# A query's weight rest and statistics placed ahead of a group of context rests on VectorE (cross attention over a long context, one core)

## The reference

```python
ln_out = _ln(hidden_states, ln_w, ln_b)
q  = _ln(_fp8_linear(ln_out, wq));  k = _ln(_fp8_linear(ln_out, wk));  v = _fp8_linear(ln_out, wv)
core = _gqa(q, k, v)                       # 16 query heads, 8 key heads, over the 64 own tokens
qx = _ln(_fp8_linear(ln_out, wqx))
kx, vx = split(einsum('bsi,oi->bso', cond, w_kv_x))   # cond: 1601 context rows
kx = _ln(kx)
xout = _gqa(qx, kx, vx)                    # over the 1601 context rows
catq = _div_clamp_fp8(concatenate([core, xout]), proj_smooth)
return einsum('bsi,oi->bso', catq, wproj) * (proj_in_scale * proj_w_scale)
```

## Time and profile before

| what | value |
|---|---|
| median of 3 runs | 1945.05 us (1943.37 to 1945.61) |
| the profiled execution, its own time | 1945.92 us |
| its span | 1944.6 us |
| TensorE busy | 1869.5 us, 96% |
| VectorE, ScalarE, GpSimd busy | 1187.0 (61%), 910.9 (47%), 731.2 us (38%) |
| attention loop, first to last score product | 138 to 1699 us, some 24.4 us a step |

### The profile page before, as it was taken

How to read it: one execution, slowest core, us unless ns; L and a number is a source line. 1 busy time by engine, 2 the same in 40 slices (tenths; PEclk the granted TensorE clock), 3 DMA queues, 4 the chain that set the end, 5 groups by cost and what they waited for, 6 DMA issues and landing times.

```text
span 1944.6 us, 31175 instructions
## 1 busy us (share of the span) xinstructions
PE 1869.5 (96%) x10065; PEld 1588.2 (82%) x10065; DVE 1187.0 (61%) x3161; ACT 910.9 (47%) x1892; POOL 731.2 (38%) x806
## 2 busy tenths in 40 slices
PE   6899999999999999999999999999999999998968
PEld 5777888888888888888888888888888888875357
DVE  7765566656565566556655765566556755546853
ACT  6653444545554555444544554455445544335611
POOL 4236554433333333334444444444444344301010
PEclk9999999999999999999999999999999999999979
DMA  8674354534453454435453544455435533474020
GB/s 276 228 251 144 106 157 133 175 114 145 149 173 120 123 171 141 152 91 178 131 155 113 171 149 140 117 175 160 142 114 180 162 114 103 154 255 165 3 87 22
DMA packets 221890, 283.82 MB, mean 146 GB/s; under 512 B 61025, under 2 KB 123746, under 8 KB 221730
## 3 DMA queue, kind: packets, MB, share of 16 engines
q1 hardware_dynamic: 211090, 280.86, 45.8%
q10 hardware_dynamic: 8592, 0.54, 0.3%
q0 software_dynamic: 2048, 0.43, 0.1%
HBM read 241.98 MB, written 39.22 MB: 145 GB/s over the span
## 4 chain that ended last, share of the span: by engine, by line
PE 78%; DVE 5%; ACT 4%; DMA 3%; issue 2%; POOL 0%; ACTq 0%; SPq 0%; DVEq 0%; POOLq 0%
PE u_ps L630 9%; PE kx_ps L524 8%; PE u_ps L633 8%; PE kx_ps L526 8%; PE kx_ps L528 8%; PE u_ps L632 8%; PE t_ps L616 4%; DMA stage<-in_ctx_n 3%; PE sc_ps L601 3%; PE sc_ps L603 2%; PE sc_ps L602 2%; PE ssq_ps L543 2%; PE t_ps L657 2%; PE t_ps L640 1%; DVE ctxN_lo L298 1%
## 5 line engine op out<-in xcount | busy, mean ns | idle before, releaser
L524 PE MATMUL kx_ps<-ctxT_hi,wk_hi 128*128 128x400 f32 (+1 forms) x1024 | 364.6, 356 | 5.5 <-DVE ctxT_lo L298 5.5
L526 PE MATMUL kx_ps<-ctxT_lo,wk_hi 128*128 128x400 f32 (+1 forms) x1024 | 354.5, 346 | 0.0
L528 PE MATMUL kx_ps<-ctxT_hi,wk_lo 128*128 128x400 f32 (+1 forms) x1024 | 353.4, 345 | 0.0
L630 PE MATMUL u_ps<-ctxN_hi,pt_hi 128*128 128x512 f32 x832 | 340.6, 409 | 6.9 <-DVE pt_lo L855 6.9
L633 PE MATMUL u_ps<-ctxN_hi,pt_lo 128*128 128x512 f32 x832 | 329.0, 395 | 0.0
L632 PE MATMUL u_ps<-ctxN_lo,pt_hi 128*128 128x512 f32 x768 | 304.4, 396 | 0.0
L855 DVE TENSOR_TENSOR pt_lo<-t_ps,pt_hi 128x512 fp32r<-128x512 f32 (+1 forms) x256 | 144.6, 588 | 242.2 <-ACT pt_hi L1120 242.2
L1089 ACT ACTIVATE kx_hi<-kx_ps 128x400 fp32r<-128x400 f32 (+1 forms) x256 | 128.8, 503 | 304.7 <-PE kx_ps L528 303.1
L1120 ACT ACTIVATE pt_hi<-t_ps 128x512 fp32r<-128x512 f32 (+1 forms) x256 | 126.0, 524 | 254.6 <-PE t_ps L616 254.5
L782 DVE TENSOR_TENSOR kx_lo<-kx_ps,kx_hi 128x400 fp32r<-128x400 f32 (+1 forms) x256 | 146.7, 573 | 151.5 <-ACT sq L1091 149.8
L524 PEld LDWEIGHTS kx_ps<-ctxT_hi,wk_hi 128*128 128x128 f32 x1024 | 193.8, 189 | 10.9 <-DVE ctxT_lo L298 6.0
(11 more groups left out here) (286 smaller groups left out, 3663.0 us busy)
## 6 DMA issues: line engine op xcount, KB each, us to landing
rstd_bc<-scratch_rstd SPq DMA_DIRECT2D x64, 804.0 KB, 6.0
stage<-in_ctx_n SPq DMA_DIRECT2D x104, 256.0 KB, 6.4
stage<-in_ctx_t SPq DMA_DIRECT2D x96, 267.0 KB, 4.6
wk_hi<-scratch_wk_s SPq DMA_DIRECT2D x56, 256.0 KB, 3.0
wk_lo<-scratch_wk_s SPq DMA_DIRECT2D x56, 256.0 KB, 3.5
wv_hi<-scratch_wv_s SPq DMA_DIRECT2D x56, 256.0 KB, 4.9
wv_lo<-scratch_wv_s SPq DMA_DIRECT2D x56, 256.0 KB, 5.8
scratch_own_rows<-out_sb SPq DMA_DIRECT2D x32, 256.0 KB, 2.8
```

The costliest lines, as they stand in the source:

```text
L524: PE.matmul(kx_ps[:, j % 2, 0:w], wk_hi[:, g % 2, i, :], ctxT_hi[:, i, c0:c0 + w], start=(i == 0), stop=False)
L526: PE.matmul(kx_ps[:, j % 2, 0:w], wk_hi[:, g % 2, i, :], ctxT_lo[:, i, c0:c0 + w], start=False, stop=False)
L528: mm = PE.matmul(kx_ps[:, j % 2, 0:w], wk_lo[:, g % 2, i, :], ctxT_hi[:, i, c0:c0 + w], start=False, stop=(i == C - 1))
L630: PE.matmul(u_ps[:], pt_hi[:, t % 2, cols], ctxN_hi[:, y, :], start=(y == 0), stop=False)
```

## The change

In VectorE's list of a step the call `refill(1)`, the rests of the pieces of place 1, moves behind the block with `query_low(n + 1)` and `query_stats(n + 2)`. It still stands in front of `values_out(n)`. The lists of the other engines are not changed.

```diff
                 if v:
                     prob_low(n, 2)
                     prob_low(n, 3)
-                refill(1)
                 if v and s:
                     query_low(n + 1)
                     if r:
                         query_stats(n + 2)
+                refill(1)
                 if v:
                     values_out(n)
                 if s:
```

## The result

| what | before | after |
|---|---|---|
| median of 4 runs each | 1945.33 us (1943.37 to 1945.84) | 1934.24 us (1932.30 to 1935.96) |
| ratio, 95% interval | 1 | 0.9949 (0.9936 to 0.9961) |
| the profiled execution, own time and span | 1945.92, 1944.6 us | 1935.84, 1933.8 us |
| last value product of n = 0 to that of n = 62 | 1529.16 us | 1518.06 us |

What follows compares the result with a forecast made beforehand. TensorE, busy in 96% of the span, was taken as the bound, so only its waits could be saved. Term 1 (-8.9) and terms 2 and 3 (-3.2) made -12.1 us, for a median of 1933.0 us, range 1928.5 to 1938.0.

Steps and rivals of the forecast that it cites:

- Rival A: Own forecast for the loop: `q_lo` waits go, steps n % 8 = 0 gain a little; 1933.0 us, chance 0.57.
- Term 1: Steps n % 8 = 5 or 7: first score product no longer waits for `q_lo`, `u_sb` not late; -8.9 us.
- terms 2 and 3: Steps n % 8 = 0: fewer `pt_lo` waits less new stalls, -7.3 + 3.8 = -3.5, taken as -3.2 us.
- Rival D: Steps n % 8 = 5 or 7: next VectorE user holds the step, nothing gained; 1945 us, chance 0.10.
- Term 2: Earlier statistics and `rstd_bc` load land the awaited context piece earlier, ending `pt_lo` waits at n % 8 = 0; up to -7.3 us.
- Term 3: Steps n % 8 = 0: last context piece's rest, behind `query_low`, makes TensorE wait; at most +3.8 us.
- part 2: Same as Term 2: earlier statistics, `rstd_bc` and awaited piece; bounds 0 and -7.3 us.
- signs of being wrong: Rests start later than ScalarE's copies allow, awaited piece keeps its landing time, or `q_hi` slips at n % 8 = 0.
- B: Only the `q_lo` gain in steps n % 8 = 5 or 7 works; 1936.1 us, chance 0.18.
- C: Gains of -8.9 and -7.3 us in full, `q_hi` in time at every n % 8 = 0; 1928.9 us, chance 0.08.
- E: Slower: at n % 8 = 0 `query_low` holds VectorE until `q_hi`, 2.2 us each; 1951.6 us, chance 0.07.

Runs made afterwards that it cites:

- low_only: Against the kernel before, only `query_low` moves ahead of the rests of place 1, `query_stats` stays behind them; 1941.28 us, ratio 0.9969.
- stats_only: Against the kernel before, only `query_stats` moves ahead of the rests of place 1, `query_low` stays behind them; 1943.19 us, ratio 0.9982.
- stats_last: The change, but with n % 8 of 5 or 7 `query_stats` goes behind the second scaling of scores; 1958.74 us, 1.0063 of the kernel before.
- rstd_later_old: Kernel before, with SyncE's `rstd_bc` load behind the piece of place 5 at n % 8 = 7 and in the entry step; 1936.39 us, ratio 0.9963.
- rstd_later: The change, plus SyncE's `rstd_bc` load behind the piece of place 5 at n % 8 = 7 and in the entry step; 1930.43 us, ratio 0.9921.
- own_behind: The change, plus GpSimd's `own_norm` moved behind `query_high` of the next step; 1930.07 us, 0.9932 of the kernel before.
- not_zeros: The change everywhere but in steps with n % 8 = 0, which keep the old order; 1934.36 us, 0.9937 of the kernel before.
- all_four: The change with `rstd_later` (not in the entry step), `make_later` and `own_behind` together; 1927.31 us, 0.9917 of the kernel before.
- zeros_only: Against the kernel before, the new order only in steps with n % 8 = 0; 1946.54 us, ratio 1.0004.
- make_later: The change, plus VectorE's first `ternary_make` moved behind later rests in odd steps from n = 29; 1932.83 us, 0.9943 of the kernel before.

## Why the prediction was right

**Time.** 1933.0 us was forecast, from 1928.5 to 1938.0; 1934.24 us was measured. Rival A held. Term 1, four fifths of the gain, came out by its mechanism and its size; that terms 2 and 3 came out near in their sum was luck.

**Term 1, -8.9 us: right in size, -8.83.** Its steps are those of the rows: `q_lo` 2.3 us ahead, the statistics inside the idle time, the rests unmoved, `u_sb` at +0.43. The two steps that I had taken 0.4 us off for, n = 23 and 29, stand at 3.25 and 3.30 us where the others take 3.03 to 3.06. What I had not seen is that the statistics carry 3.9 us of it. My sum was right, since it counted TensorE's whole delay against n = 22; my reading of the wait, as one for `q_lo` alone, was not, and `low_only`, for which I expected 8.8, showed it. Even when `q_lo` is early, statistics that stand behind the rests keep `u_sb` late by 0.4 us. Rival D is refuted by the same rows.

**Term 2, up to -7.3 us: the mechanism is shown, the size was too large.** `stats_only` and `stats_last` show the chain from the statistics over GpSimd, `rstd_bc` and SyncE's queue to the piece awaited in the zero; `rstd_later_old` shows its last link alone. But 7.3 us was more than there is: with every wait out of the zeros Z is -6.3. The 0.26 us that I put on top of each wait came from one wait of a score product, and the zeros don't have it: their seven waits for `pt_lo` and three that I had not counted, for the squares of the keys (0.25 to 0.49 us in n = 8, 16 and 24), are 6.5 us as noted, of which 6.3 come back. And the step "so the piece should land about 2 us earlier against TensorE" held in four zeros (2.1 to 2.3 us in n = 8, 16, 24 and 56) and not in n = 32, 40 and 48 (0.8, 1.2 and 0.9 us), where ScalarE still idles for 1.9 to 2.2 us and not for less than 0.5. `rstd_bc` was to be issued 5.3 us after the last value product in the sevens and is issued after 6.0 to 7.4 us. Two things took the lead away. First `q_n`, in all sevens and fives: it takes 0.80 us in every step of the loop before, and 1.53 to 1.88 us in the 14 fives and sevens after. There, and only there, it runs while VectorE takes the context rests (533.77 to 535.06 in n = 15). By the Trainium skill, "SBUF — State Buffer", section "Who interferes with whom", this is what a VectorE instruction with two SBUF inputs does to GpSimd; the trace agrees in part: `q_n` is 0.73 to 1.08 us longer, in n = 15 0.74 us over an overlap of 1.0 us, where I had given 1.3 us as the upper case. Second, the small store of the key norms lands later in n = 31, 39 and 47 (3.3, 2.7 and 3.2 us after its issue), the sevens ahead of just those three zeros, and in no other seven; the transfers in a short window around it, in n = 31 (the packets of each queue: number, MB, share; then KB each and us from issue to landing) and in n = 15:

```profile
q8 instruction: 1, 0.02, 1.6%
...
scratch_rstd<-rstd_col POOLq DMA_DIRECT2D x1, 6.5 KB, 3.3
```

```profile
scratch_rstd<-rstd_col POOLq DMA_DIRECT2D x1, 6.5 KB, 1.8
```

3.3 us against 1.8 us from issue to landing, and `rstd_bc` waits for it: 7.42 us after the last value product in place of 6.01. Why it lands late is not shown by an experiment (below).

**Term 3, +3.8 us: the mechanism is right, the size was too large.** The wait of a value product for the piece's rest exists, in one zero (1.0 us, n = 56), and in five when the transfers are helped (`rstd_later`). `own_behind` puts what `q_hi` takes back after the change at 1.6 us at most, 0.9 of it in n = 56; `not_zeros` doesn't tell the cost of the order from nothing. It was smaller for two reasons. In n = 32, 40 and 48 part 2 gave less, as I had allowed for. And n = 8, which I had counted with the late ones, is not of their kind after the change: `q_hi` comes 0.7 us earlier against TensorE's keys there, and the piece's rest follows ScalarE's copy. One of my signs of being wrong was that `q_hi` slips in the zeros; in n = 56 it did, by 0.4 us. Two terms too large of opposite sign made a net that is near by cancelling: -3.2 us forecast for 2 and 3, -3.05 measured. That net is luck.

**The remaining rivals.** B (only part 1) is refuted by `stats_only`; in the four late zeros the change comes close to it, 0.56 us of gain. C is about what `all_four` reaches in the loop (-8.87 - 6.32), by three more edits and not by itself. E's place, `query_low` ahead of the last piece in the zeros, is there, but `zeros_only` and `not_zeros` show at most 0.3 us for it in sum, and not 1.8 us a zero. The other places lost 0.8 us. The largest are 0.63 us from n = 61 to 62 and 0.58 us from n = 12 to 13, where a wait of 0.5 us for `pt_lo` is new; both scatter from kernel to kernel (the second from 0.1 to 1.1 us).

## What to carry to other kernels

When two independent instructions of an in-order engine move together, ask for each of them who waits for it: here the one read as the cause brought 4.9 us, the small one behind it 3.9 us more where it stood and up to 6 us three engines and one step further on. A result that another engine turns into a transfer belongs ahead of work that nobody awaits, and its lateness is not symmetrical: 2.7 us earlier brought 3 to 6 us in the zeros, 1.5 us later (2.1 us against TensorE) cost 16. When a wait ends because something comes earlier, look up what is due next in that step (`q_hi` here) before counting the whole wait as gain.

## What the runs showed that I had not expected

- **The same GpSimd instruction took twice the time behind the start of a context rest:** `q_n` 0.80 us in all steps of the loop before, 1.53 to 1.88 us in the 14 steps where it starts while one runs. In `stats_only` it starts 0.2 us ahead of the rests in n = 23 and 29; there it takes 0.80 us, and the first of the two rests takes 0.80 us against 0.68 and 0.70 for the second. The 14 take 22.5 us together where 14 x 0.80 = 11.2 us would do, which is 11.3 of the 14.7 us by which GpSimd's busy time grew.
- **A 6.5 KB store issued by GpSimd lands after 1.8 us, or up to 4.0 us after its issue.** In the loops of the kernel before, the change, `stats_only` and `make_later` it landed later than 2.0 us in 30 of the 33 cases in which a packet of an instruction-fetch queue was recorded 0.9 to 1.5 us after the issue, and in 47 of the 215 cases without such a packet. No experiment tried it; it stays an observation.
- **The last value product of n = 0 comes 163.7 to 169.1 us after the start** in the eleven profiled executions whose edit does not act in the entry step, while an undisturbed step of the loop repeats to 0.05 us. The sum of A and Z, read from start times, is steadier than single times; the late zeros and a few other steps still scatter by up to 1 us each.
